# A macaron block on one core: the DMA transpose of the split tile, in one piece in place of two

## The chip, the cores and the metric

One core of a Trainium2 chip runs the kernel. The metric is the device time of one execution in microseconds, as the median of several runs. Beside it stands one execution recorded by the hardware profiler, from which all rows come.

## The reference

The input x has 2 sequences of 2048 tokens of width 256. The block is a feed-forward, a Mamba-like state space layer, and the same feed-forward again, each on a layer-normalised input and added to x:

```python
x = x + 0.5 * ffn(layernorm(x), w_gate, w_up, w_down)
x = x + attn(layernorm(x), in_proj_w, conv_w, ..., out_proj_w)
x = x + 0.5 * ffn(layernorm(x), w_gate, w_up, w_down)
# ffn: (silu(x @ wg.T) * (x @ wu.T)) @ wd.T, weights are int / 127, hidden 768
# attn: xz = x @ in_proj.T; causal conv of 4 taps on xc; delta, B from xc @ x_proj.T;
#       h = A_bar * h + B_bar along the tokens; (h @ C.T + xc * D) * silu(z) @ out_proj.T
```

## The kernel before, in words

All five engines run their own program, written out by hand and joined by semaphores. The tokens are cut into tiles of 512 (four blocks of 128), and the two sequences alternate: one half step h works on one tile of one sequence, and `half(g)` of each engine is the program of a half step. In half step h part B is the state space layer on the tile of sequence `g.b`; part C is the second feed-forward of the tile that part B finished in the half step before (sequence `g.f`), and part A is the first feed-forward of the next tile of the same sequence `g.f`. Half steps 1 to 6 have all three parts; part A of half steps -1 and 0 belongs to the start-up.

Matmuls take float16 operands: a value is multiplied by 256 and split into a high half and a low half, and the two are multiplied separately. For parts B and C the normalised tile XN is transposed by TensorE (`turn_norm`, line 1540) and then split. For part A of half steps 1 to 6 it goes the other way round: XN is split first, into `XS16` (128 tokens x 4 blocks x high or low x 256), and a DMA transpose brings `XS16` into `XT` with the width on the partitions. The steps of this path are:

- VectorE, `normalize(g, "A", ...)`, line 900: one block of XN each; blocks 0 and 1 early in the half step, blocks 2 and 3 after the last `hidden` of part C.
- ScalarE, `split_hi` (line 566): the high halves of blocks 0, 1 (j = 0) and of blocks 2, 3 (j = 1), each raises `s_hi`. Before j = 0 it waits until the transposes of the half step before have landed (`turned`).
- VectorE, `split_lo` (line 913): the low halves, j = 0, then `delta_in` of part B, then j = 1; each raises `s_lo`.
- SP (lines 382 to 390): waits for `s_hi` and `s_lo` of j, issues the DMA transpose of these two blocks, then the same for the next two.
- TensorE, `gate_up` (line 1577): before the first gate product of part A it waits until everything has landed (`turned`), line 1583; then 12 products of four matmuls each read `XT`.

A transpose of two blocks is 128 x 1024 elements of 2 bytes, 256 KB. SP's queue in a half step is, in this order: the load of the next tile of x (line 381), the two transposes, and the two stores of part C's result (line 396). SP also waits at line 384 until the last part A no longer reads `XT`. TensorE's order is the table `ORDER` (line 62): the last up product of part C, x_proj (xp0, xp1) of part B, the four down groups of part C, then gate and up of part A, c_proj, down of part A, out_proj, and the transposes of the normalised tile for the next part B. All matmuls of products are recorded at line 1566, TensorE's transposes at line 1471.

```python
XS16 = sb("xs16", [P, NB, 2, D], F16)
XT = sb("xt", [P, NB, 2, KD, P], F16)
```

Of the kernel before, what the change touches and what calls it, by code (L numbers as in the profile page):

```python
# [183 lines left out]
def wait(eng, sem, value):  # L184

    if not isinstance(value, int) or value > 0:
        eng.wait_ge(sem, value)


def macaron(nc, x, in_w, conv_w, conv_b, xp_w, dt_w, dt_b, a_log, d_skip, c_w, out_w, wg, wu, wd, out):  # L190
    with ExitStack() as ctx:
        def sb(name, shape, dt=F32):
            return ctx.enter_context(nc.sbuf_tensor(name, shape, dt))
# [4 lines left out]
        def sem(name):  # L198
            return ctx.enter_context(nc.semaphore(name))
# [17 lines left out]
        XS16 = sb("xs16", [P, NB, 2, D], F16)  # L217
        XT = sb("xt", [P, NB, 2, KD, P], F16)
# [36 lines left out]
        A = sb("a", [P, 1])  # L255
# [77 lines left out]
        s_hi, s_lo, turned = sem("s_hi"), sem("s_lo"), sem("turned")  # L333
# [14 lines left out]
        def xrows(s, t):  # L348
            return x[s, bass.ds(t * TILE, TILE), :].rearrange("(b p) d -> p b d", p=P)

        def orows(s, t):
            return out[s, bass.ds(t * TILE, TILE), :].rearrange("(b p) d -> p b d", p=P)
# [4 lines left out]
        @block.sync  # L357
        def _(sp):
            sp.dma_start(XPRE[0][:, :, :], xrows(0, 0)).then_inc(ld_x[0], 16)
            for j in range(HC // 2):  # L360
                sp.dma_start(NGI[:, 2 * j:2 * j + 2, :], wg[2 * P * j:2 * P * (j + 1), :]
                             .rearrange("(c p) f -> p c f", p=P)).then_inc(ld_g[j], 16)
            sp.dma_start(NDI, wd.rearrange("(a p) h -> p a h", p=P)).then_inc(ld["d"], 16)
            sp.dma_start(XPRE[1][:, :, :], xrows(1, 0)).then_inc(ld_x[1], 16)
            sp.dma_start(NI, in_w.rearrange("(c p) f -> p c f", p=P)).then_inc(ld["i"], 16)
            sp.dma_start(NX, xp_w[RANK:RANK + N, :]).then_inc(ld["x"], 16)
            sp.dma_start(XPD, xp_w[0:RANK, :]).then_inc(ld["dt"], 16)
            sp.dma_start(DTN[:, :], dt_w).then_inc(ld["dt"], 16)
            sp.dma_start(CW[:, :, :], conv_w.rearrange("(m p) o k -> p m (o k)", p=P)).then_inc(ld["small"], 16)
            sp.dma_start(CB[:, :], conv_b.rearrange("(m p) -> p m", p=P), allow_slow_non_contiguous=True).then_inc(ld["small"], 16)  # L370
            sp.dma_start(DS[:, :], d_skip.rearrange("(m p) -> p m", p=P), allow_slow_non_contiguous=True).then_inc(ld["small"], 16)
            sp.dma_start(DTB[:, :], dt_b.rearrange("(p o) -> p o", o=1)).then_inc(ld["small"], 16)
            sp.dma_start(AL[:, :], a_log.rearrange("(p o) -> p o", o=1)).then_inc(ld["small"], 16)
            sp.dma_start(NC, c_w.rearrange("(m p) n -> p m n", p=P)).then_inc(ld["c"], 16)
            sp.dma_start(NO, out_w.rearrange("(a p) i -> p a i", p=P)).then_inc(ld["o"], 16)

            def half(g):
                if g.has("A") and g.h > 0:

                    sp.wait_ge(res_done, 2 * g.number("token", "A", back=2) + 2)  # L380
                    sp.dma_start(XPRE[g.f][:, :, :], xrows(g.f, g.tile("A"))).then_inc(ld_x[g.f], 16)
                if g.has("A") and g.h > 0:
                    if g.h > 1:
                        sp.wait_ge(h_ready, HC * g.number("ffn", "A", back=1) + HC)
                    for j in range(2):
                        sp.wait_ge(s_hi, 2 * g.number("split", "A") + j + 1)
                        sp.wait_ge(s_lo, 2 * g.number("split", "A") + j + 1)
                        sp.dma_start_transpose(  # L388
                            XT[:, 2 * j:2 * j + 2, :, :, :].rearrange("p b s k t -> p (b s k) t"),
                            XS16[:, 2 * j:2 * j + 2, :, :].rearrange("p b s d -> p (b s d)")).then_inc(turned, 16)  # L390
                if g.has("C"):

                    for j in range(2):
                        blocks = slice(2 * j, 2 * j + 2)
                        sp.wait_ge(res_done, 2 * g.number("token", "C") + j + 1)
                        sp.dma_start(orows(g.f, g.tile("C"))[:, blocks, :], X[g.f][:, blocks, :])\
                            .then_inc(st_y[g.f], 16)

            for h in range(1, LAST + 1):
                half(Half(h))  # L400
            for s in S2:
                sp.wait_ge(st_y[s], 32 * STEPS)
# [94 lines left out]
        def _(act):  # L497
# [68 lines left out]
            def split_hi(g, halves):  # L566

                for j in halves:
                    act.wait_ge(xn_ready, 2 * g.number("norm", "A") + j + 1)
                    if j == 0:  # L570
                        wait(act, turned, 32 * g.number("split", "A"))
                    act.activation(XS16[:, 2 * j:2 * j + 2, 0, :], XN[:, 2 * j:2 * j + 2, :], ACT.Copy, scale=XS)\
                        .then_inc(s_hi, 1)

# [76 lines left out]
            def half(g):  # L651
# [41 lines left out]
                if A and g.h > 0:  # L693
                    split_hi(g, (0,))
                if C:
                    hidden_high(g, "C", (5,))
                if A and g.h > 0:
                    split_hi(g, (1,))
# [768 lines left out]
        def _(pe):  # L1467
# [83 lines left out]
            def split_waits(g, k, low, back=0):  # L1551


                n = g.number("turn", k, 1, back)
                return {kc: (t_hi[kc], n) for kc in range(KD)} | {low + kc: (t_lo[kc], n) for kc in range(KD)}
# [13 lines left out]
            def product(g, what, part, terms, more=(), waits={}):  # L1569

                who, count = g.before(what, part)
                if who:
                    pe.wait_ge(readers[who], count)
                bank = g.bank(what, part)[0]
                accumulate(q[bank][:, :], terms, more, flags[0], waits).then_inc(q_full[bank], 1)

            def gate_up(g, k, what):
                up, c = what[0] == "u", int(what[-1])
                w1, w2, w3 = (WU, WU2, WU3) if up else (WG, WG2, WG3)

                by_dma = k == "A" and g.h > 0
                if by_dma and c == up == 0:
                    pe.wait_ge(turned, 32 * g.number("split", "A", 1))

                def moving(part, kc):
                    return XT[:, :, int(part is XL), kc, :] if by_dma else part[g.f][:, kc, :]

                def terms(*pairs):
                    return [(w[:, kc, P * c:P * (c + 1)], moving(part, kc)) for w, part in pairs for kc in range(KD)]
                product(g, what, k, terms((w1, XH), (w1, XL)), terms((w2, XH), (w3, XH), (w2, XL)),  # L1590
                        waits=split_waits(g, k, KD) if c == up == 0 and not by_dma else {})
# [47 lines left out]
            def do(what, part, h):  # L1639
                g = Half(h)  # L1640
                if what == "fill":
                    fill(part)
                elif what[:-1] == "count":
                    count_over(int(what[-1]))
                elif what[:-1] == "flag":
                    flags[int(what[-1])] = flag_value(int(what[-1]))
                elif what[:-1] == "more":
                    n = int(what[-1])
                    further_parts(flags[n], [p for p in PARTS if (p[0] == "d") == n])
                elif what == "bound":  # L1650
                    bound()
                elif what == "dtn":
                    turn_rank()
                elif what[:-1] == "turn":
                    turn_norm(g, part, int(what[-1]))
                elif what[:-1] in ("gate", "up"):
                    gate_up(g, part, what)
                elif what[:-2] == "down":
                    down(g, part, int(what[-2]), (int(what[-1]),))
                elif what[:-1] in ("ix", "iz"):  # L1660
                    in_proj(g, what)
                elif what[:-1] == "xp":
                    x_proj(g, int(what[-1]))
                elif what[:-1] == "cp":
                    c_proj(g, int(what[-1]))
                else:
                    out_proj(g, int(what[-2]), (int(what[-1]),))
# [35 lines left out]
```

## Time and profile before

| what | us |
|---|---|
| median of 3 runs | 539.74 |
| lowest and highest | 536.33, 540.13 |
| the profiled execution | 536.74 |
| its span, first to last instruction | 534.9 |
| mean granted TensorE clock in it | 0.984 |

Times in the rows are microseconds from the start of the span, unless they are marked ns. The profiled execution's own time is 1.8 us longer than its span.

### The profile page before, as it was taken

To read this page: it belongs to the slowest core of one execution; us is meant where nothing else is said; L and a number is where in the kernel's file an instruction comes from. 1 tells how busy PE (TensorE), PEld (TensorE's weight loads), DVE (VectorE), ACT (ScalarE), POOL (GpSimd) and SP (SyncE) were. 2 spreads that over 40 slices of the span, in tenths; PEclk is the share of its full clock that TensorE was granted. 3 is DMA by queue.
4 is the path that set the end of the run, shared out by engine and by line. 5 is a ranking of instruction groups with operands and counts; after the bars stand their busy time and mean duration, and the time that the engine had idled before them with its cause. 6 is when DMAs were issued, how large, how long until landed. Compare 5 with 4: busy or idle time off the path is not lost.

```text
span 534.9 us, 7722 instructions
## 1 busy us (share of the span) xinstructions
PE 499.3 (93%) x2657; PEld 291.1 (54%) x2657; DVE 415.5 (78%) x865; ACT 280.0 (52%) x472; POOL 226.8 (42%) x192
## 2 busy tenths in 40 slices
PE   2788988999999999999999999999999999999586
PEld 2456436646584557545574557545574547545434
DVE  4788997897879876997879876997789876887332
ACT  5383961477408761576418660576318760575032
POOL 1132237154733736162723646162824636063322
PEclk9699999999999999999999999999999999999979
DMA  8401000002010022002010112003110111000001
GB/s 291 127 0 43 1 0 2 0 2 42 21 60 2 5 37 80 1 2 41 31 51 1 12 31 80 1 2 42 40 39 3 19 24 40 1 1 21 20 2 40
DMA packets 27240, 16.84 MB, mean 31 GB/s; under 512 B 15264, under 2 KB 26528, under 8 KB 27184
## 3 DMA queue, kind: packets, MB, share of 16 engines
q1 hardware_dynamic: 26368, 15.26, 11.1%
q8 instruction: 40, 0.66, 0.5%
q10 hardware_dynamic: 816, 0.79, 0.5%
q14 instruction: 16, 0.13, 0.1%
HBM read 8.71 MB, written 4.19 MB: 24 GB/s over the span
## 4 chain that ended last, share of the span: by engine, by line
PE 70%; DVE 13%; DMA 5%; issue 4%; ACT 4%; POOL 2%; SPq 2%; POOLq 0%; ACTq 0%; DVEq 0%
PE q L1566 47%; PE dp L1566 19%; DMA xt<-xs 3%; PE tp L1471 3%; DVE xn L900 3%; DVE h L930 2%; DVE xs L917 1%; SPq L388 1%; DVE xc L955 1%; DMA hh<-in_L_ffn_w_gate_dram 1%; POOL hl L427 1%; DVE x L941 1%; ACT xc L558 1%; DVE hs L1012 1%; ACT sg L582 0%
## 5 line engine op out<-in xcount | busy, mean ns | idle before, releaser
L427 POOL TENSOR_TENSOR hl<-h,hh 128x512 f16<-128x512 f32 x96 | 121.2, 1277 | 108.3 <-ACT hh L590 108.1
L930 DVE SCALAR_TENSOR_TENSOR h<-sg,hsm,q 128x512 f32<-128x512 f32 x96 | 70.6, 742 | 37.6 <-PE q L1566 24.9
L955 DVE SCALAR_TENSOR_TENSOR xc<-xi,cw,xc 128x512 f32<-128x512 f32 x96 | 84.7, 898 | 0.5
L564 ACT ACTIVATE xh<-tp 128x512 f16<-128x512 f32 x36 | 19.7, 598 | 116.5 <-PE tp L1471 116.5
L582 ACT ACTIVATE sg<-q 128x512 f32<-128x512 f32 x96 | 56.7, 591 | 39.4 <-PE q L1566 39.4
L590 ACT ACTIVATE hh<-h 128x512 f16<-128x512 f32 x96 | 60.2, 629 | 29.0 <-DVE h L930 28.8
L434 POOL TENSOR_TENSOR xcl<-xc,xch 128x512 f16<-128x512 f32 x32 | 40.8, 1283 | 49.2 <-ACT xch L615 49.2
L1566 PE MATMUL dp<-wo,yu 128*128 128x256 f32 x256 | 58.6, 381 | 1.5 <-POOL yu L442 1.5
L1566 PE MATMUL dp<-wd,hl 128*128 128x256 bf16 x384 | 52.9, 273 | 2.7 <-POOL hl L427 2.7
L1566 PE MATMUL dp<-wd,hh 128*128 128x256 bf16 x384 | 52.7, 273 | 1.0 <-ACT hh L590 0.9
L1566 PEld LDWEIGHTS dp<-wo,yu 128*128 128x128 f32 x256 | 47.2, 190 | 9.1 <-POOL yu L442 2.7
L1566 PEld LDWEIGHTS dp<-wd,hh 128*128 128x128 f16 x384 | 37.4, 98 | 12.6 <-issue 4.6
L442 POOL TENSOR_TENSOR yu<-yu,sz 128x512 f32<-128x512 f32 x32 | 39.7, 1275 | 8.7 <-DVE yu L1026 8.6
L1566 PEld LDWEIGHTS dp<-wd,hl 128*128 128x128 f16 x384 | 37.5, 98 | 7.9 <-issue 3.5
L1566 PE MATMUL q<-xh,wg 128*128 128x512 f16 x120 | 37.6, 396 | 3.2 <-DVE xl L909 2.6
L600 ACT ACTIVATE xc<-q,cb,rw 128x512 f32<-128x512 f32 x32 | 24.9, 779 | 28.9 <-PE q L1566 28.8
L1566 PE MATMUL q<-xt,wg 128*128 128x512 f16 x144 | 37.0, 380 | 1.9 <-DMA xt<-xs 1.9
L1566 PE MATMUL q<-xl,wih 128*128 128x512 f16 x128 | 38.2, 379 | 0.0
L1566 PE MATMUL q<-xh,wih 128*128 128x512 f16 x128 | 38.1, 379 | 0.0
L1566 PE MATMUL q<-xh,wil 128*128 128x512 f16 x128 | 38.1, 379 | 0.0
L1566 PE MATMUL q<-xl,wg 128*128 128x512 f16 x120 | 37.6, 394 | 0.0
L1566 PE MATMUL q<-xh,wu 128*128 128x512 f16 x120 | 36.7, 388 | 0.7 <-ACT sg L582 0.7
(184 smaller groups left out, 847.2 us busy)
## 6 DMA issues: line engine op xcount, KB each, us to landing
xpre<-in_L_attn_x_dram SPq DMA_DIRECT2D x8, 512.0 KB, 4.6
out_dram<-x SPq DMA_DIRECT2D x16, 256.0 KB, 2.1
xc<-in_L_attn_in_proj_w_dram SPq DMA_DIRECT2D x1, 1024.0 KB, 10.9
hl<-in_L_ffn_w_up_dram ACTq DMA_DIRECT2D x3, 256.0 KB, 6.3
hh<-in_L_ffn_w_gate_dram SPq DMA_DIRECT2D x3, 256.0 KB, 6.8
hh<-in_L_ffn_w_down_dram SPq DMA_DIRECT2D x1, 768.0 KB, 8.1
yu<-n_L_attn_out_proj_w_dram SPq DMA_DIRECT2D x1, 512.0 KB, 4.7
yu<-in_L_attn_x_proj_w_dram SPq DMA_DIRECT2D x1, 256.0 KB, 11.0
```

What stands on the lines that cost most here:

```text
L427: pool.tensor_tensor(HL[g.f][:, c, :], H[:, j, :], HH[g.f][:, c, :], ALU.subtract)\
L434: pool.tensor_tensor(XCL[:, m, :], XC[g.b][:, m, :], XCH[:, m, :], ALU.subtract)\
L442: pool.tensor_tensor(YU[g.b][:, m, :], YU[g.b][:, m, :], SZ[g.b][:, m, :], ALU.mult)\
L564: act.activation(XH[g.f][:, kc, :], tp[kc][:, :], ACT.Copy, scale=XS).then_inc(t_hi[kc], 1)
L582: act.activation(SG[:, (first + c) % 2, :], q[bank][:, :], ACT.Silu, scale=QUANT / XS)\
L590: act.activation(HH[g.f][:, c, :], H[:, (first + c) % 3, :], ACT.Copy).then_inc(hh_ready, 1)
L600: act.activation(XC[g.b][:, m, :], q[bank][:, :], ACT.Identity, bias=CB[:, m:m + 1], scale=RW3[:, m:m + 1]).then_inc(xc_begun, 1)
L900: ins = dve.tensor_scalar(XN[:, b, :], src[:, b, :], MN[k][:, b:b + 1], RS[k][:, b:b + 1], ALU.subtract, ALU.mult)
L930: dve.scalar_tensor_tensor(out=H[:, first % 3, :], in0=SG[:, first % 2, :], scalar=HSM[:, c:c + 1], in1=q[bank][:, :], op0=ALU.mult, op1=A ...
L955: dve.scalar_tensor_tensor(out=XC[s][:, m, :], in0=XI[s][:, m, k:k + TILE], scalar=CW[:, m, k:k + 1], in1=XC[s][:, m, :], op0=ALU.mult, op ...
L1471: return pe.transpose(dst, src, IDN[:, :] if ident is None else ident)
L1566: ins = pe.matmul(out, w, a, start=(at == 0), stop=(at == len(terms) - 1))
```

## The change

SP waits until both halves of the split (high and low, of all four blocks) are made and issues one DMA transpose of the whole `XS16` into the whole `XT`, in place of two transposes of two blocks each. The landing raises `turned` by 16 a half step and no longer by 32, and the two waits for `turned` count accordingly.

```diff
--- before.py
+++ after.py
@@ -382,12 +382,10 @@
                 if g.has("A") and g.h > 0:
                     if g.h > 1:
                         sp.wait_ge(h_ready, HC * g.number("ffn", "A", back=1) + HC)
-                    for j in range(2):
-                        sp.wait_ge(s_hi, 2 * g.number("split", "A") + j + 1)
-                        sp.wait_ge(s_lo, 2 * g.number("split", "A") + j + 1)
-                        sp.dma_start_transpose(
-                            XT[:, 2 * j:2 * j + 2, :, :, :].rearrange("p b s k t -> p (b s k) t"),
-                            XS16[:, 2 * j:2 * j + 2, :, :].rearrange("p b s d -> p (b s d)")).then_inc(turned, 16)
+                    sp.wait_ge(s_hi, 2 * g.number("split", "A") + 2)
+                    sp.wait_ge(s_lo, 2 * g.number("split", "A") + 2)
+                    sp.dma_start_transpose(XT[:, :, :, :, :].rearrange("p b s k t -> p (b s k) t"),
+                                           XS16[:, :, :, :].rearrange("p b s d -> p (b s d)")).then_inc(turned, 16)
                 if g.has("C"):
 
                     for j in range(2):
@@ -568,7 +566,7 @@
                 for j in halves:
                     act.wait_ge(xn_ready, 2 * g.number("norm", "A") + j + 1)
                     if j == 0:
-                        wait(act, turned, 32 * g.number("split", "A"))
+                        wait(act, turned, 16 * g.number("split", "A"))
                     act.activation(XS16[:, 2 * j:2 * j + 2, 0, :], XN[:, 2 * j:2 * j + 2, :], ACT.Copy, scale=XS)\
                         .then_inc(s_hi, 1)
 
@@ -1580,7 +1578,7 @@
 
                 by_dma = k == "A" and g.h > 0
                 if by_dma and c == up == 0:
-                    pe.wait_ge(turned, 32 * g.number("split", "A", 1))
+                    pe.wait_ge(turned, 16 * g.number("split", "A", 1))
 
                 def moving(part, kc):
                     return XT[:, :, int(part is XL), kc, :] if by_dma else part[g.f][:, kc, :]
```

## Rows read from the trace of the kernel before

**Rows 1.** Page: busy time of the engines, and the chain's shares by line.
```profile
PE 499.3 (93%) x2657; PEld 291.1 (54%) x2657; DVE 415.5 (78%) x865; ACT 280.0 (52%) x472; POOL 226.8 (42%) x192
...
PE q L1566 47%; PE dp L1566 19%; DMA xt<-xs 3%; PE tp L1471 3%; DVE xn L900 3%; DVE h L930 2%; DVE xs L917 1%; SPq L388 1%; DVE xc L955 1%; DMA hh<-in_L_ffn_w_gate_dram 1%; POOL hl L427 1%; DVE x L941 1%; ACT xc L558 1%; DVE hs L1012 1%; AC
```

**Rows 2.** Chain that ended last, half step 4: start us, us, what.
```profile
301.24 2.42 DVE xn L900 x2
303.66 1.57 DVE xs L917
305.31 1.24 SPq L388
306.64 3.69 DMA xt<-xs
310.38 13.97 PE q L1566 x56
```

**Rows 3.** The same chain, SP's first transpose and TensorE's start, half steps 2, 3, 5, 6.
```profile
185.74 1.83 SPq L388
...
190.84 13.97 PE q L1566 x56
...
245.33 2.28 SPq L388
...
250.81 13.97 PE q L1566 x56
...
364.89 1.24 SPq L388
...
370.24 13.97 PE q L1566 x56
...
424.74 1.24 SPq L388
...
429.82 7.09 PE q L1566 x32
```

**Rows 4.** Timeline of half step 1: both transposes (start us, us, engine), TensorE's start.
```profile
126.58 2.69 SPq L388 DMA_TRANSPOSE xt<-xs  x2
...
131.26 1.03 PE L1566 MATMUL q<-xt,wg 128*128 128x512 f16 x4
```

**Rows 5.** Timeline of half step 2: the two operations of split_lo.
```profile
184.01 1.65 DVE L917 SCALAR_TENSOR_TENSOR xs<-xn,xs 128x512 f16<-128x512 f32 x1
...
186.24 0.68 DVE L917 SCALAR_TENSOR_TENSOR xs<-xn,xs 128x512 f16<-128x512 f32 x1
```

**Rows 6.** Line 388: in half step 1 (ns min/median/max; landing), then all waits for it.
```profile
L388 SPq DMA_TRANSPOSE xt<-xs x2: 1272/1294/1315, 126.6 to 128.0; - x2
...
DMA to landing us min/median/max: 3.1/3.2/3.3
...
  PEld q L1566: 3.2, 5
```

**Rows 7.** Windows: us, engines' busy us (x), PEclk, DMA share, GB/s; half steps 1, 2, 4.
```profile
126.60:127.80 1.20, 1.20 (x14) 1.07 (x12) 1.15 (x2) 0.90 (x2) 0.00 (x0) 1.00 0.00 0
127.80:129.00 1.20, 1.20 (x14) 1.07 (x12) 0.30 (x1) 0.83 (x2) 0.00 (x0) 1.00 1.01 191
...
187.00:187.40 0.40, 0.40 (x6) 0.35 (x5) 0.00 (x0) 0.37 (x2) 0.00 (x0) 1.00 1.02 209
...
307.20:308.00 0.80, 0.80 (x10) 0.72 (x8) 0.54 (x2) 0.30 (x2) 0.00 (x0) 1.00 0.57 14
...
308.20:308.40 0.20, 0.20 (x4) 0.18 (x3) 0.18 (x1) 0.20 (x1) 0.00 (x0) 1.00 1.26 284
```

**Rows 8.** DMA queue of instructions (packets, MB, share), windows 186.0:186.2 and 366.6:366.7.
```profile
q8 instruction: 1, 0.02, 30.9%
...
q8 instruction: 1, 0.02, 59.1%
```

**Rows 9.** Page: DMA issues, the store of part C (KB each, median us to landing).
```profile
out_dram<-x SPq DMA_DIRECT2D x16, 256.0 KB, 2.1
```

## The prediction

> **What bounds the kernel now.** I read the page's busy times and chain first: TensorE is busy for 499.3 of 534.9 us, and most of the chain that ended last is its own matmuls, but 3% of it is the landing of the transpose xt<-xs and 1% its issue on SP [rows 1]. So the transpose sits on the path. The chain in order of time shows how [rows 2]. In each half step the chain leaves TensorE after the last up product of part C: VectorE makes h, normalises two blocks of xn (2.42), makes the low half xs of the first two token blocks (1.57), SP issues the first transpose (1.24) and right behind it the second, which lands 3.69 us after its issue began, and TensorE's first gate product of part A starts 0.05 us later. Meanwhile TensorE only has x_proj and the down products of part C to do, and it runs out of them shortly before the landing: its weight loads waited 3.2 us for this transfer, in five of the six half steps that have one [rows 6]. In the first of the six it didn't wait. All that TensorE does between one such landing and the next excursion is in order and without a gap in the chain, so a landing that comes x later makes the half step x longer, and one that comes earlier can give back no more than those 3.2 us altogether.
>
> **What the change does to this chain.** Before, the first transpose starts when the first two blocks are split, the second follows as soon as SP has finished the first. After, nothing starts until all four blocks are split, and then one transpose of twice the size goes out. The terms, from SP's first issue (t = 0) to TensorE's start:
>
> *Later start, early half.* The two split_lo operations end at 184.01 + 1.65 = 185.66 and 186.24 + 0.68 = 186.92 [rows 5], 1.26 us apart, since delta_in stands between them. The new issue so starts at t = 1.26. The old second issue starts at about t = 1.24 + 0.10 = 1.34 where SP is not held up [rows 2]. The start of the last issue hardly moves (0.08 us earlier); what is lost is the head start of the first half. ScalarE's high halves are done long before, so the two waits moved together add none; behind them on SP's queue stand only the stores of part C, due many microseconds later. Six fewer issues and twelve fewer waits on SP cost and save nothing in themselves.
>
> *Landing of the whole.* A half took 1.27 to 1.32 us to issue and 3.1 to 3.3 us from issue to landing in half step 1, where nothing disturbed it [rows 6]. A plain store of 256 KB landed after 2.1 us [rows 9], so a transpose of 256 KB pays about a microsecond for being one. The windows divide the 3.1: no data moved between 126.6 and 127.8, the first 1.2 us after the issue began; then 191 GB/s flowed over the next 1.2 us, its first ramp included [rows 7], so that the 256 KB take about 1.25 us; the rest of the 3.1, some 0.65, is the tail. 256 KB in 1.25 us is 210 GB/s, the pace at which SP issues (256 KB in 1.24 to 1.3 us). But after a pause in half step 4 the same engines moved 284 GB/s for a moment [rows 7]. [...] No row shows a transpose of another size, so its price is bounded: below by a landing that takes no longer than a half's does (3.1), above by two whole halves one after the other (6.2). I take a fixed 1.2 plus tail, and twice the 1.25: 3.1 + 1.25 = 4.35 us. It is nearest to the rows, as issue pace and data pace are equal in them.
>
> [...]
>
> *Sum without disturbance.* TensorE would start at t = 1.26 + 4.35 + 0.05 = 5.66. SP's first issues began at 126.58, 185.74, 245.33, 305.31, 364.89 and 424.74, TensorE's starts were 131.26, 190.84, 250.81, 310.38, 370.24 and 429.82 [rows 2 to 4], so t = 4.68, 5.10, 5.48, 5.07, 5.35, 5.08. The new start is later by 0.98, 0.56, 0.18, 0.59, 0.31 and 0.58 us: together 3.2.
>
> *What goes away: a pause in the middle of the transposes.* Half steps 2 to 6 are 0.4 to 0.8 us slower than the first for a reason that the windows show. Data flow, then almost stop (14 GB/s over 307.2 to 308.0), then go on [rows 7]. In each of these five half steps, and not in the first, a 16 KB instruction packet starts on one of the 16 DMA engines 0.4 to 1.8 us after SP's first issue: at 186.0 to 186.2 with 0.309 x 16 x 0.2 = 0.99 us, the earliest by this measure, and at 366.6 to 366.7 with 0.591 x 16 x 0.1 = 0.95 us, the latest, of five [rows 8]. [...] The new transpose's data begin only at t = 1.26 + 1.2 = 2.46, when four of the five packets are over; that is already in the sum above, whose 4.35 has no pause in it. In half step 5 the packet ends near 367.6 and data would begin at 367.35, so a pause of some 0.4 us stays there. That makes 3.2 + 0.4 = 3.6 us.
>
> *Against the profiled execution* (536.74 us, span 534.9) this is 540.3. The median of the three runs is 539.74, 3.0 above the profiled one; put onto the median the forecast is 543.3 us, 0.7% more. A measurement of this kernel can tell about 1%, 5.4 us, from no change, so the likeliest verdict is no change, on the slow side.
>
> **Rivals.**
> A, *size is nearly free*: SP's issue is not what paces the data, and the whole flows at the engines' own rate. At the 284 GB/s of half step 4, 512 KB take 1.85 us, the landing 1.2 + 1.85 + 0.65 = 3.7, TensorE's start t = 1.26 + 3.7 + 0.05 = 5.01. Against the six old starts that is +0.33, -0.09, -0.47, -0.06, -0.34, -0.07: 0.7 us less in all, 539.0 on the median. For it: the engines were faster behind the pause. Against: undisturbed data never were, though in half step 1 the second half's descriptors could have queued up. [...]
> [...]
> C, *two phases in the issue*, the rival on the slow side: SP first prepares the whole transpose and data begin only when it is done, at 1.2 us now because a half's issue lasts 1.24. Then both the 1.2 and the 1.25 double, the landing takes 3.1 + 2.45 = 5.55 and each of the six starts is 1.2 later than in my sum: 3.2 + 7.2 = 10.4 us, 550.1, 1.9% slower. It decides wherever the first data wait for the end of the issue. For it: the first data and the end of the issue coincide in half step 1. Against: in half step 2 SP's issue ran from 185.74 to 187.57 by the chain [rows 3], and data moved at 209 GB/s from 187.0 on [rows 7].
> D, *the compiler or SP still makes two of it*: both would then go out back to back at t = 1.26, landing at the same 4.35 or a little later; this is no other time than mine.
>
> **How the numbers follow.** My forecast has 0.62, A 0.14, B 0.13, C 0.10, and 0.01 is left. Range: 538 (A with a margin; my forecast on the lower of the three runs is 540) to 549 (B with a margin, and most of the way to C). Slower by over 1%: C, half of B, and a tenth of my own case, 0.10 + 0.07 + 0.07 = 0.24. Faster by over 1% would need more than the 3.2 us that TensorE waits: 0.03. Within 1%: 0.73.
>
> **What would show it.** In the profile of the changed kernel: six transposes with an issue of about 2.5 us each (A: much under 2; the same 1.3 would break my sum) and a landing of 4.2 to 4.6 us; first data 1.2 us after the issue began (C: 2.4); the issue 1.3 us later against the end of the first split_lo; TensorE's idle time on xt<-xs up from some 0.5 us to 1 us or more a half step, and now in half step 1 too; no pause at 10 GB/s, except in half step 5 (B: in five). The time between TensorE's starts on xt should be nearly even, with half steps 1 and 2 growing most. I am wrong if the landing isn't near 4.35, or if TensorE's later start is made up again before the next excursion of the chain.

## The result, and the profile after

The changed kernel takes 540.40 us, the kernel before 537.71 us (medians of 19 runs each); the ratio is 1.0056, with a 95% interval of 1.0037 to 1.0074. That is 3.0 us slower by the ratio (2.7 us between the medians), a little over half a per cent. One run of the kernel before took 1063.76 us, for a reason that nothing here shows, and is set aside. The forecast was 3.6 us. (The three runs of before that stood ahead of the prediction had a median of 539.74; with more runs it is 2.0 us lower, and most of the 2.9 us by which the predicted 543.3 us is too high comes from that.)

The page of the changed kernel, where line numbers are two lower, answers to [rows 1]:

```profile
span 537.6 us, 7710 instructions
...
PE 497.8 (93%) x2657; PEld 291.2 (54%) x2657; DVE 416.4 (77%) x865; ACT 280.0 (52%) x472; POOL 226.7 (42%) x192
...
PE q L1564 46%; PE dp L1564 18%; DMA xt<-xs 5%; PE tp L1469 3%; DVE xn L898 3%; DVE xs L915 2%; DVE h L928 2%; DVE xc L953 1%; DMA hh<-in_L_ffn_w_gate_dram 1%; POOL hl L425 1%; DVE sp L967 1%; ACT xc L556 1%; DVE x L939 1%; DVE hs L1010 1%;
```

TensorE's work is what it was; the landing xt<-xs holds 5% of the chain in place of 3, and SP's issue has left it, since the chain counts a landing from the start of its own issue. The view of line 387, the transpose, answers to [rows 6]: duration of the issue (min/median/max in ns), who waited for it (us, times), and the time from issue to landing.

```profile
L387 SPq DMA_TRANSPOSE xt<-xs x6: 1323/1986/2522, 129.2 to 429.8; - x6
...
  PEld q L1564: 6.2, 6
...
DMA to landing us min/median/max: 4.3/4.3/4.4
```

Six transposes, and their landings take the same time within 0.1 us, 4.3 to 4.4 us. Their issues don't: 1.32 to 2.52 us. TensorE's weight loads now wait 6.2 us for them, in all six half steps, where they waited 3.2 us in five. The difference is 3.0 us, as much as the result. The agreement is partly luck: the two profiled executions are 2.7 us apart in span, and they also differ where the change does nothing. In the changed one the first split of half step 1, which the change can't have touched, ends 1.4 us later, and the stretch from TensorE's last start on xt to the end is 1.6 us shorter. The chain that ended last (start us, us, what), in half step 4 with its split, and with TensorE's starts on xt:

```profile
129.21 4.35 DMA xt<-xs
133.61 13.97 PE q L1564 x56
...
193.72 13.97 PE q L1564 x56
...
253.78 13.97 PE q L1564 x56
...
306.63 1.56 DVE xs L915
...
308.85 0.61 DVE xs L915
309.54 4.27 DMA xt<-xs
313.86 13.97 PE q L1564 x56
...
373.97 13.97 PE q L1564 x56
...
434.10 7.09 PE q L1564 x32
```

The reader is to see two things. First, in half step 4 the split of the first two blocks ends at 308.19, that of the second two at 309.46, the transpose starts at 309.54 and TensorE at 313.86: t = 5.59 after the moment (308.27) at which the kernel before would have issued its first transpose. In all six half steps t is 5.67, 5.62, 5.58, 5.59, 5.64 and 5.60. Second, the spacing of TensorE's starts is 60.11, 60.06, 60.08, 60.11 and 60.13 us. Before, it was 59.58, 59.97, 59.57, 59.86 and 59.58 [rows 2 to 4]. What varied from half step to half step has gone, at a higher level. The windows of half step 2 (columns as in [rows 7]) show the transfer:

```profile
189.37:190.40 1.03, 1.03 (x12) 0.92 (x11) 0.17 (x1) 0.80 (x2) 0.00 (x0) 1.00 0.00 0
190.40:193.00 2.60, 2.56 (x24) 2.04 (x21) 2.46 (x5) 2.26 (x3) 0.00 (x0) 1.00 1.03 197
193.00:193.30 0.30, 0.00 (x0) 0.00 (x0) 0.30 (x1) 0.30 (x1) 0.00 (x0) 1.00 0.23 43
```

There is nothing for 1.03 us, then 197 GB/s on average over the 2.6 us of the data, then the tail. No landing is longer than 4.35 us, so no pause is left in any half step.

### The profile page after: what moved, and what is told of

Same layout as the page of the kernel before. It is cut to its first block, busy times and chain, and to the rows that moved or that the text cites. A ratio compares the mean times of both kernels' runs of the same rounds, so it can differ in the third digit from the quotient of the medians.

```text
span 537.6 us, 7710 instructions
## 1 busy us (share of the span) xinstructions
PE 497.8 (93%) x2657; PEld 291.2 (54%) x2657; DVE 416.4 (77%) x865; ACT 280.0 (52%) x472; POOL 226.7 (42%) x192
## 4 chain that ended last, share of the span: by engine, by line
PE 68%; DVE 16%; DMA 6%; issue 4%; ACT 4%; POOL 2%; POOLq 0%; SPq 0%; ACTq 0%; DVEq 0%
PE q L1564 46%; PE dp L1564 18%; DMA xt<-xs 5%; PE tp L1469 3%; DVE xn L898 3%; DVE xs L915 2%; DVE h L928 2%; DVE xc L953 1%; DMA hh<-in_L_ffn_w_gate_dram 1%; POOL hl L425 1%; DVE sp L967 1%; ACT xc L556 1%; DVE x L939 1%; DVE hs L1010 1%; ACT sg L580 0%
## 5 line engine op out<-in xcount | busy, mean ns | idle before, releaser
L588 ACT ACTIVATE hh<-h 128x512 f16<-128x512 f32 x96 | 60.2, 629 | 29.2 <-DVE h L928 29.0
```

The costliest lines, as they stand in the source:

```text
L588: act.activation(HH[g.f][:, c, :], H[:, (first + c) % 3, :], ACT.Copy).then_inc(hh_ready, 1)
```

## Experiments

The terms below are those of the prediction: t counts from the moment at which the kernel before issues its first transpose, and a TensorE that doesn't wait for xt starts at t = 4.68. Ratios are to the kernel before, run on the same chip; the experiments ran on three chips, so ratios of different ones compare only roughly. The spacing is the time between TensorE's first xt products of two half steps, from the timelines; without a wait it is 59.16 us.

### Two transposes, both late

```diff
-                        sp.wait_ge(s_hi, 2 * g.number("split", "A") + j + 1)
-                        sp.wait_ge(s_lo, 2 * g.number("split", "A") + j + 1)
+                        sp.wait_ge(s_hi, 2 * g.number("split", "A") + 2)
+                        sp.wait_ge(s_lo, 2 * g.number("split", "A") + 2)
```

> Two transposes as before, but both wait for all four blocks to be split. Theory (lost head start; the data of 256 KB take 1.25 us, wherever they stand): SP issues at t = 1.26 and 2.6 after the first split, the second lands 3.1 us later, TensorE starts at t = 5.75, within 0.2 us a half step of the changed kernel: about 0.6 to 0.8% slower than before. Rival (one large transpose costs less than two, and the change only lost what it gave up in head start): TensorE starts a microsecond or more later than in the changed kernel in each of six half steps, 1.7% slower than before or more.

Measured: 541.59 us, ratio 1.011 (1.0064 to 1.0157). Its view of the transpose line:

```profile
L388 SPq DMA_TRANSPOSE xt<-xs x12: 1237/1268/1315, 127.2 to 430.2; - x12
...
  PEld q L1566: 7.7, 6
...
DMA to landing us min/median/max: 3.1/3.2/3.3
```

Every half lands 3.1 to 3.3 us after its issue, and nothing pauses. The second issue starts 1.34 us after the first, so TensorE starts some 0.2 us later than in the changed kernel in most half steps (spacing 60.28 to 60.50), and its weight loads wait 7.7 us in place of 6.2. The ratio is higher than these 1.5 us ask for, but its interval holds them; the times alone don't tell this kernel from the changed one, the profile does. The change is thereby taken apart: waiting for all four blocks is the loss, and making one transpose of the two gives a small part of it back, 0.2 to 0.4 us of the 1.1 to 1.3 by which TensorE starts late in each half step.

### Four transposes of one block each

```diff
-                        sp.dma_start_transpose(
-                            XT[:, 2 * j:2 * j + 2, :, :, :].rearrange("p b s k t -> p (b s k) t"),
-                            XS16[:, 2 * j:2 * j + 2, :, :].rearrange("p b s d -> p (b s d)")).then_inc(turned, 16)
+                        for b in (2 * j, 2 * j + 1):
+                            sp.dma_start_transpose(
+                                XT[:, b:b + 1, :, :, :].rearrange("p b s k t -> p (b s k) t"),
+                                XS16[:, b:b + 1, :, :].rearrange("p b s d -> p (b s d)")).then_inc(turned, 16)
```

(and 64 in place of 32 in the two waits for `turned`)

> Four transposes of one block each (128 KB) in each half step, the first two after the first split, the last two after the second. If the price goes by bytes (issue 0.65 us, landing 1.2 + 0.63 + 0.65 = 2.5 us), the last one lands at t = 2.0 + 2.5 = 4.5, 0.1 us earlier than undisturbed halves: same as before or 0.2% faster. If each issue costs 1.3 us whatever its size, the last issue begins at t = 4.0 and lands at 6.5: 1.9 us later in each of six half steps, some 11 us less the pauses, 1.5 to 2% slower.

Measured: 549.89 us, ratio 1.024 (1.0196 to 1.0285).

```profile
L389 SPq DMA_TRANSPOSE xt<-xs x24: 1201/1264/2593, 127.1 to 441.5; - x24
...
DMA to landing us min/median/max: 2.4/2.5/4.3
```

Here is a piece of the prediction that falls. An issue costs SP 1.20 us or more for 128 KB as for 256 KB (1.24 with two late transposes), and the changed kernel's shortest, for 512 KB, is 1.32 us: it doesn't go by size in proportion. (The others of 512 KB took 1.81 to 2.52 us. Why, no run shows: the first of them took 2.00 us with no packet of instructions near it.) The landing does grow with the size, and so there are now three sizes: 2.5 us for 128 KB, 3.1 for 256, 4.3 for 512. These three fit a fixed part of 1.9 us and 0.6 us for each 128 KB. Four issues in a row are the bound here:

```profile
188.12 5.90 SPq L389 DMA_TRANSPOSE xt<-xs  x4
...
195.29 1.08 PE L1567 MATMUL q<-xt,wg 128*128 128x512 f16 x4 [2.33 <-DMA xt<-xs]
```

SP is at it for 5.9 us (the first of the four took 1.98 us; by the trace a packet of instructions starts 0.4 us after its beginning), and TensorE waits 2.33 us. The time is somewhat above the estimate (2.4% in place of 1.5 to 2); TensorE's clock has a part in it, which is told further down, with the changed kernel moved by 128 places.

### The changed kernel with the second split ahead of delta_in

```diff
                     normalize(g, "A", (2, 3))
-                    split_lo(g, (0,))
+                    split_lo(g, (0, 1))
                 if B:
                     delta_in(g)
-                if A and g.h > 0:
-                    split_lo(g, (1,))
```

> The changed kernel with the second low half made right behind the first, ahead of part B's first step (delta_in), so that the last split ends some 0.66 us earlier. Theory (TensorE's start hangs on the end of the last split plus 4.35 us): every half step 0.6 to 0.7 us shorter, 4 us less than the changed kernel, ratio to before about 0.998. Rival (delta_in and the steps behind it are as late as the transpose, or the landing is set by something else): no more than 1 us is won back.

Measured: 537.40 us, ratio 1.0008 (0.9984 to 1.0032), 2.6 us less by its ratio than the changed kernel. It was to be 4 us. The landings of half steps 1, 2, 4 and 5 by the chain say why:

```profile
127.04 4.34 DMA xt<-xs
...
186.53 4.28 DMA xt<-xs
...
305.36 4.91 DMA xt<-xs
...
365.42 5.00 DMA xt<-xs
```

In half steps 1 to 3 the transpose lands after 4.3 us and the spacing falls to 59.4 us, 0.7 less, as the theory has it. In half steps 4 to 6 it lands after 4.9 to 5.0, since its data begin 0.7 us earlier and pause again. The windows of half step 4:

```profile
306.50:307.20 0.70, 0.70 (x9) 0.63 (x7) 0.00 (x0) 0.67 (x2) 0.00 (x0) 1.00 1.84 176
307.20:308.10 0.90, 0.90 (x10) 0.81 (x9) 0.58 (x2) 0.40 (x2) 0.00 (x0) 1.00 0.63 9
```

176 GB/s, then 9 GB/s for 0.9 us. By the trace, a packet of instructions starts 0.4, 1.1 and 1.1 us after the issue in half steps 4, 5 and 6; in half steps 2 and 3 it starts 0.2 and 0.1 us before it, and there is no pause. The last split does set the start, and the pause depends on the moment and not on the number of transposes: one transpose has it too, where a packet starts 0.4 to 1.1 us after its issue.

### The same swap in the kernel before

> The kernel before with the second low half made right behind the first, ahead of delta_in. The quarters showed an issue of 1.2 us whatever the size, so in the kernel before the second transpose waits for SP's first issue (1.24 + 0.1 us), not for the second split (1.26). Theory: the split that ends 0.66 us earlier changes nothing there, SP's two issues stay 1.34 us apart, ratio to before 0.998 to 1.002. Rival (the second split sets the start): 0.6 us a half step less, 3 us, ratio 0.994.

Measured: 539.05 us, ratio 1.0009 (0.9986 to 1.0032). In the chain of half step 4 SP's first issue starts at 306.77, takes 1.24 us, and the second transpose starts at 308.11, 1.34 us after the first, just as before, though its blocks were ready 0.7 us earlier. In the kernel before, SP's own issue time keeps the second transpose back. But the swap isn't without effect, though the time doesn't show it. In half step 1, where TensorE doesn't wait for xt, it now waits for the scan of part B, and the next start on xt comes 1.05 us later than it did (60.63 us in place of 59.58). The pauses of half steps 4 to 6 are also longer: the second transpose lands after 4.00 to 4.31 us, where it took 3.69 to 3.96. Together these are some 2 us; the ratio's interval holds 1.7.

### TensorE's program moved by 64 places

By the trace a packet of instructions starts 0.4 to 1.7 us after SP's first issue in each half step with a pause ([rows 8] has the first and the latest). There are 40 on this queue, of 16 KB each by the page of the kernel before (packets, MB, share):

```profile
q8 instruction: 40, 0.66, 0.5%
```

Whether these packets cause the pause is tried by 64 waits more at the start of TensorE's program, which leave its work as it is and may move them:

```diff
         def _(pe):
-            pe.wait_ge(idn_ready, 1)
+            for _ in range(65):
+                pe.wait_ge(idn_ready, 1)
```

> The kernel before with 64 waits more at the very start of TensorE's program (all met at once), so that every place of its program lies 64 instructions further and the 16 KB instruction packets of TensorE are fetched up to 5 us earlier. Theory (the packet on one DMA engine causes the pause in the transposes): the pauses of half steps 2 to 6 go, the second transpose lands 3.1 to 3.3 us after its issue everywhere, TensorE waits under 0.5 us in all for xt: 2.7 us less, ratio 0.995. Rival (the pause belongs to two transposes close behind each other, or to something else on the chip): five pauses as before, ratio 1.000.

Measured: 537.30 us, ratio 1.0014 (0.9991 to 1.0038): no gain, and by its time a miss. The profile says more. Half step 2, in the view of the transpose line of that stretch:

```profile
L388 SPq DMA_TRANSPOSE xt<-xs x2: 1237/1262/1287, 185.4 to 186.8; - x2
...
DMA to landing us min/median/max: 3.1/3.1/3.2
```

Its pause is gone; before, its first transpose was issued over 1.83 us and TensorE started at t = 5.10 [rows 3]. But half steps 3 to 6 still had one, with landings of up to 4.14 us by the chain:

```profile
365.26 4.14 DMA xt<-xs
...
425.28 3.69 DMA xt<-xs
```

By the trace, the packets of these four half steps start 0.4 to 1.1 us after the first issue. That of half step 2 starts at 182.4, 3.0 us ahead of the issue; before, it started at 186.1, 0.4 us behind it. So the waits do move the packets.

### Moved by 128 places

> The kernel before with 128 waits more at the start of TensorE's program in place of 64. With 64 the packet near the transposes left half step 2 alone (no pause, landings of 3.1 and 3.2 us), while half steps 3 to 6 kept one. Theory (the packets are TensorE's, and a pause comes exactly where one of them overlaps the transposes): the set of half steps with a packet close to the first transpose changes again, most likely half steps 2 and 3 are free, and landings over 3.4 us stand only in half steps with such a packet. Rival (the packets belong to another engine, the change in half step 2 was chance): the same half steps as with 64 or as before. In time under 1.5 us either way.

Measured: 534.62 us, ratio 0.9938 (0.9914 to 0.9961). Only half steps 5 and 6 kept a pause. The wait for xt and the landings of the whole execution:

```profile
  PEld q L1567: 1.1, 2
...
DMA to landing us min/median/max: 3.1/3.2/3.9
```

The DMA view of half step 4 (302 to 308 us), which has no packet of instructions:

```profile
q1 hardware_dynamic: 2112, 0.52, 45.5%
issues: line engine op xcount, KB each, median us to landing
xt<-xs SPq DMA_TRANSPOSE x2, 3.2
```

and a line of the same view of half step 5 (361.9 to 366.9 us), which has one and paused:

```profile
q8 instruction: 1, 0.02, 1.2%
```

TensorE's starts are 59.16, 59.16, 59.15, 59.52 and 59.71 us apart. Three states of the same program (unmoved, by 64, by 128) have their pauses in half steps 2 to 6, 3 to 6 and 5 to 6, each time exactly where a packet starts close to the transposes: by the trace 0.4 to 1.8 us after the first issue. In the half steps without a pause none starts from 2.8 us before that issue to 3.8 us after it. Only TensorE's program was moved, and packets and pauses moved with it, so I take the packets for TensorE's and for the cause of the pause. TensorE's weight loads wait 1.1 us in place of 3.2 [rows 6], so the vanished pauses account for 2.1 of the 3.3 us. The rest isn't placed. SP's first issue of half step 1 stands 1.2 us earlier in this profile than before (125.38 against 126.58), but the profiles of kernels with the same start-up scatter by more: the first split ends at 125.83 with two late transposes and at 127.86 in the changed kernel.

### The changed kernel moved by 128 places

> The changed kernel with the same 128 waits at the start of TensorE's program. It has no pause to lose, so this is the control for the kernel before with 128 waits, which came out at 0.994 where its vanished pauses account for 1.8 us or 0.997. Theory: the waits are worth something of their own only in the start-up (TensorE's first xt product stood 1.2 us earlier there), so this kernel keeps its landings of 4.3 us and its 0.9 us of TensorE waits a half step, and lies between 1.003 and 1.006. Rival (moving the packets helps wherever they fall, by shorter fetches elsewhere in the half steps): the spacing of TensorE's starts drops under 60.0 us, ratio 1.000 or less.

Measured: 541.14 us, ratio 1.0069 (1.0044 to 1.0094), with spacings of 60.04 to 60.16 us from half step 2 on. From half step 1 to 2 it is 62.06 us. The profiled execution, the slowest of the six runs (542.86 us), shows why in the chain and the windows (PEclk is the third column from the end):

```profile
127.14 6.15 DMA xt<-xs
...
133.34 15.65 PE q L1565 x56
```

```profile
127.00:133.20 6.20, 3.72 (x35) 3.09 (x32) 3.47 (x7) 3.86 (x6) 0.00 (x0) 1.00 0.45 87
...
133.40:136.80 3.40, 3.40 (x9) 1.20 (x10) 0.00 (x0) 1.18 (x2) 0.00 (x0) 0.50 0.00 0
```

The landing took 6.15 us here, TensorE was idle for 2.6 us, and then its granted clock stood at 0.50 (its records in the traces are 1.00 or 0.50) for 3.4 us of dense work, whose 56 matmuls took 15.65 us in place of 13.97. The data weren't late: by the trace all but the last of them had flowed by 131.1. But the move put a packet of instructions right there, at 131.28, and the landing came 2.0 us after the packet's start. The DMA view of 131 to 133.3 us has it:

```profile
q8 instruction: 1, 0.02, 2.5%
```

In half step 2 a packet starts at 194.60, and the landing took 4.59 us. So in the two half steps in which a packet starts 4.1 and 3.8 us after the issue the landing is late, 6.15 and 4.59 us in place of 4.3; whether the packet holds it up wasn't tried.

The control is therefore not clean. It shows no gain from the waits themselves, but it has disturbances of its own, so it can't rule out that they are worth a microsecond or two elsewhere. Set against the kernel before moved likewise (on another chip, so only roughly) the changed kernel is slower by 1.0069 / 0.9938 = 1.013, or 7 us. Part of that are these disturbances; without any pause on either side, the six later starts of the changed kernel make 5.6 us (t = 5.58 to 5.67 against 4.68).

The quarters show the lower clock as well, and that the length of the idle time alone doesn't decide. After 2.33 us in half step 2 the clock was 0.57 on average from 197 to 200 us, and half steps 2 and 3 stood 1.7 us further apart than the waits explain; after 2.41 us in half step 6 it was 0.50. After 2.22 us in half step 3, 2.07 in half step 4 and even 2.85 in half step 5 it stayed at 1.00. The timeline and the window of half step 5:

```profile
382.25 1.04 PE L1567 MATMUL q<-xt,wg 128*128 128x512 f16 x4 [2.85 <-DMA xt<-xs]
382.40:385.80 3.40, 3.40 (x17) 1.56 (x16) 0.75 (x1) 2.00 (x4) 0.12 (x1) 1.00 0.00 0
```

### Split by high and low

The high halves of all blocks are made 0.9 us before the first low half. With high and low outermost in `XS16` and `XT`, one transpose takes all high halves and the other all low ones (the operations that write `XS16` and the products that read `XT` follow the new order, which isn't shown):

```diff
-        XS16 = sb("xs16", [P, NB, 2, D], F16)
-        XT = sb("xt", [P, NB, 2, KD, P], F16)
+        XS16 = sb("xs16", [P, 2, NB, D], F16)
+        XT = sb("xt", [P, 2, NB, KD, P], F16)
...
+                    for s in range(2):
+                        sp.wait_ge((s_hi, s_lo)[s], 2 * g.number("split", "A") + 2)
+                        sp.dma_start_transpose(
+                            XT[:, s:s + 1, :, :, :].rearrange("p s b k t -> p (s b k) t"),
+                            XS16[:, s:s + 1, :, :].rearrange("p s b d -> p (s b d)")).then_inc(turned, 16)
```

> Two transposes of 256 KB again, but one of all high halves and one of all low halves (the tiles XS16 and XT are laid out with high and low outermost). The high halves of all blocks are ready 0.9 us before the first low half, so the first issue no longer stands in the way of the second, which starts at t = 1.26 and lands 3.1 us later: TensorE could start at t = 4.41, and is itself ready at 4.68. Theory: TensorE waits for xt less than 0.2 us a half step except where a packet falls into the second transpose's data, 2.5 us less than before, ratio 0.995, and 1% less than the changed kernel. Rival (a transpose in flight delays the next, or the packet pauses come along): ratio 0.999 to 1.002.

Measured: 535.17 us, ratio 0.9948 (0.9926 to 0.9969). The view of the transpose line:

```profile
L387 SPq DMA_TRANSPOSE xt<-xs x12: 1233/1275/2139, 125.7 to 423.8; - x12
...
who waited for it (us, times):
busy tenths in 40 slices 0000000000000000000000000000000000000000
DMA to landing us min/median/max: 3.0/3.4/4.9
```

Nobody waited for it any more; the list of who waited is empty. Spacings are 59.15 to 59.21 us. The landings of up to 4.9 us are those of the high halves, which start early enough to hide them; the low halves land after 3.0 to 3.4 us. In half step 4:

```profile
303.25 4.14 SPq L387 DMA_TRANSPOSE xt<-xs  x2
...
304.66 0.68 DVE L916 SCALAR_TENSOR_TENSOR xs<-xn,xs 128x512 f16<-128x512 f32 x1
...
308.84 1.03 PE L1565 MATMUL q<-xt,wg 128*128 128x512 f16 x4
```

The first transpose is issued at 303.25, before either low half is ready; the last of these is ready at 305.34, and SP is through with both issues at 307.39. TensorE starts at 308.84 without a wait. This is faster than both kernels: 0.5% faster than before and about 1.1% faster than the changed one (0.9948 against 1.0056).

### Split by high and low, with the swap

> The same with the second low half ahead of delta_in: the last split ends at t = 0.6, the low transpose could land at 3.7, but SP's issue of the high one ends at about 0.4 to 0.5, so nothing holds it. TensorE's own work ends at 4.68, so no more than with the kernel without this swap is to be had: ratio 0.995; pauses of up to 0.9 us are now hidden too. If delta_in's delay of 0.66 us shows, the time is above that kernel's.

Measured: 538.37 us, ratio 1.0005 (0.9977 to 1.0033): the whole gain is lost again. TensorE hardly waits for xt, but the spacing is 60.2 to 60.4 us, with the last of 59.36 as the exception. TensorE now waits in the middle of part A, here in half step 1:

```profile
142.09 4.08 PE L1563 MATMUL q<-hs,wc 128*128 128x512 f32 x8 [0.41 <-DVE hs L1011]
```

It waits for the scan (hs), which comes later because the chain of part B begins with the delta_in that was moved back. In the kernel without the swap the same eight matmuls start without a wait and take 3.60 us. From the last up product to the end of these eight, half step 1 loses 1.07 us, and that is all by which its spacing grew. Part B's chain has less slack than the 0.66 us of the swap as soon as TensorE doesn't wait for xt; why 0.66 us of delay cost 1.07 isn't shown.

### Split by high and low, moved by 128 places

> The kernel by high and low halves with the 128 waits. TensorE didn't wait for xt in it any more, so the pauses were hidden and moving them wins nothing in the half steps: spacing 59.2 us as before it. If the 128 waits are worth something in the start-up, it shows here too: ratio 0.992 to 0.995, otherwise 0.995.

Measured: 533.74 us, ratio 0.9937 (0.9917 to 0.9957), spacings of 59.16 and 59.17 us throughout. It is the fastest kernel of all by its median, though its interval overlaps that of its unmoved form; whether the start-up gains by the move stays open.

## Why the prediction was right, and where it wasn't

**The chain and the later start** were right: the one issue starts 1.27 us after the moment of the old first one (1.26 in the sum), and the loss is the head start of the first half. The kernel with two late transposes shows it alone, at a little more than the change's price.

**The landing of the whole**, taken as 4.35 us, measured 4.27 to 4.35 by the chain. In half step 2 the first data came 1.03 us after the issue began, they flowed for 2.6 us and the tail took 0.67, against 1.2, 2.5 and 0.65 in the sum. The sum put TensorE's start at t = 5.66; it was 5.58 to 5.67. Against the six old starts that makes 0.99, 0.52, 0.10, 0.52, 0.29 and 0.52 us, 2.9 together, where 3.2 stood in the prediction.

**The reason given for the pace was wrong**, though the number held. I took the landing of the whole from the equality of SP's issue time and the data's time (1.24 and 1.25 us for 256 KB), as if the two went together at any size. The issue costs 1.2 to 1.3 us for 128 KB and 256 KB alike; that it equalled the data's time at 256 KB was chance, and that the landing still came out at 4.35 us was luck in this respect. The prediction had said that an issue of 1.3 us for the whole would break its sum. The six took 1.32 to 2.52 us, and the one of 1.32 us landed like the others: its issue was over at 190.69, and the data flowed on until 193.0 (197 GB/s on average from 190.4). So the issue's length doesn't set the pace, and the sum held for another reason: the landings of the three sizes, 2.5, 3.1 and 4.3 us, lie on a line, 1.9 us and 0.6 us for each 128 KB. What holds the data at about 210 GB/s no run shows.

**The pause in half step 5**, 0.4 us of the forecast 3.6, didn't come. Its packet started between 369.3 and 369.5, 1.0 to 1.2 us after the moment of the old first issue (368.33), where it had started 1.7 us after it before; the data came later still, after 370.6. In half steps 2, 3, 4 and 6 a packet started 0.4 to 1.3 us after that moment, and again before the data. The forecast had left the packets where they were. Why this one moved wasn't tried. How long a pause is for a given place of its packet, no run shows; the 0.4 us were an estimate, and in their place this half step has a landing of 4.3 us. Without this term the sum was 3.2, against 3.0.

**The rivals.** A (size is nearly free) falls with the landing of 4.3 us, where it had 3.7. C (two phases) falls too: the first data weren't later (1.03 us after the issue began, in half step 2), and they came before the end of the issue (1.32 us). B (all five half steps pause as before) was wrong for the changed kernel, but the swap shows that it was near: with the same single transpose 0.7 us earlier, three half steps of six had the pause. That the change lost only 3.0 us and not the 5.6 that six undisturbed half steps would cost is due to the pauses that the kernel before had and the later start avoids [rows 7, 8]; the moved programs confirm the cause.

## What to carry to other kernels

When two halves are joined into one transfer, what counts on a critical path is the time from the last producer to the landing: with both halves late TensorE started 1.1 to 1.3 us later in each half step than its own work asks for, and one issue in place of two gave 0.2 to 0.4 us of that back. Where a transfer's issue stands in the way of the next, as here, where the second came 1.34 us after the first, cut the work by what is ready first (high and low: ratio 0.9948), not by what is nearest in the loop. And compare the variation between like stages before and after: five half steps of six were slower than the first for a reason of their own, which decided half the size of the result.

## What the runs showed of the hardware

- The packets of instructions, 16 KB each, took 0.99 and 0.95 us of a DMA engine's time in [rows 8]. Where one started 0.4 to 1.8 us after the first issue of the kernel before, or 0.4 to 1.1 us after that of the changed kernel with the swap, the transpose's data almost stopped (14 GB/s over 0.8 us in [rows 7], 9 GB/s over 0.9 us with the swap); behind the pause of [rows 7] 284 GB/s flowed for 0.2 us. Moving TensorE's program by 128 waits took three of five such pauses away in the kernel before (ratio 0.9938). In the changed kernel the same move put a packet 4.1 us after an issue, and the landing took 6.15 us in place of 4.35.
- A DMA transpose from SBUF to SBUF cost SP 1.2 to 1.3 us at 128 and at 256 KB where nothing paused, and 1.32 to 2.52 us at 512 KB, the spread without a known cause. It landed after 2.5, 3.1 and 4.3 us, or about 1.9 us and 0.6 us for each 128 KB; at 512 KB it did so whatever the issue took. SP's issue took longer where a packet started 0.4 to 0.5 us after its beginning (1.83 and 2.28 us at 256 KB in half steps 2 and 3 of [rows 3]).
- After 2.3, 2.4 and 2.6 us without work TensorE's granted clock fell from 1.00 to 0.50 for 3.4 us, which cost 1.7 us in each of the two cases that were worked out (2.3 and 2.6 us). After 2.1, 2.2 and 2.85 us it stayed at 1.00, so the length of the idle time alone didn't decide. After the 0.7 to 0.8 us of idle time in the changed kernel's half steps it always stayed there. The late landing of 6.15 us so cost 1.7 us more than its wait.
